# A Flamingo layer with an expert lookup: searches and decoding one stage ahead of the gather, and attention values as weights

## The reference, cut to what matters

```
x = x + tanh(g_xattn) * attention(layernorm(x), ctx, Wq, Wkv, Wout)      # causal softmax, 16 heads
x = x + tanh(g_ffn) * ffn(layernorm(x), ...)

h = silu(x W_up + b_up) W_down + b_down                                  # 256 -> 1024 -> 128
q = h W_q;  sim = q . keys                                               # 2 x 8 heads x 45 keys
scores, idx = top_k(sim, 8)
sc, pk = top_k(sx[:, None] + sy[None, :], 8)                             # best 8 of 64 sums per head
indices = (ix * 45 + iy)[pk]                                             # 64 experts per token
z = silu((h . down_embed[indices]) * softmax(sc))
out = sum over the 64 of z * up_embed[indices]
```

## Time and profile before

| | |
|---|---|
| median of three runs | 1368.43 us |
| the profiled execution | 1370.69 us |
| its span on the core | 1368.9 us |
| PE busy | 1238.8 us, 90% |
| DVE busy | 1020.6 us, 75% |
| ACT busy | 653.0 us, 48% |
| POOL busy | 289.0 us, 21% |
| mean granted clock of PE | 0.955 of 2.4 GHz |

### The profile page before, as it was taken

The page is one execution under the profiler, slowest core; times in us unless marked ns, Lnnn a source line. Parts: engine busy times, 40 slices in busy tenths (PEclk is TensorE's granted clock), DMA queues, the critical chain, the costliest instruction groups (busy, mean ns, idle before and its releaser), DMA issues.

```text
span 1368.9 us, 47081 instructions
## 1 busy us (share of the span) xinstructions
PE 1238.8 (90%) x18876; PEld 1101.5 (80%) x18876; DVE 1020.6 (75%) x4298; ACT 653.0 (48%) x1866; POOL 289.0 (21%) x151
## 2 busy tenths in 40 slices
PE   5778999999999999999999999999999999999755
PEld 3666888888888888888888888888888888888644
DVE  1437878886787878778878787787888778877873
ACT  3455544554554455555454554554545545554210
POOL 1220222220122222112222220222222112222220
PEclk9989999999999999999999999999999999999968
DMA  7005433565542455555443565544345565444455
GB/s 188 6 6 130 119 91 74 120 134 134 134 122 83 75 124 134 134 134 122 106 116 65 130 134 133 134 114 112 98 81 134 134 134 129 110 112 86 106 124 123
DMA packets 300319, 153.30 MB, mean 112 GB/s; under 512 B 278111, under 2 KB 291271, under 8 KB 291911
## 3 DMA queue, kind: packets, MB, share of 16 engines
q1 hardware_dynamic: 300103, 150.29, 47.6%
HBM read 78.44 MB, written 4.72 MB: 61 GB/s over the span
## 4 chain that ended last, share of the span: by engine, by line
DVE 40%; PE 25%; DMA 21%; issue 11%; SPq 2%; ACT 1%; DVEq 0%; POOL 0%; POOLq 0%
DMA hot_rT<-expert_rows 16%; DVE uc L610 7%; PE bank L960 6%; DVE topi L702 6%; PE bank L841 4%; DMA expert_rows<-r_h 4%; DVE picked L589 3%; DVE besti L691 3%; DVE smax L617 3%; PE bank L854 2%; DVE best L682 2%; PE bank L910 2%; PE bank L864 2%; PE bank L891 2%; DVE eq L740 2%
## 5 line engine op out<-in xcount | busy, mean ns | idle before, releaser
L362 POOL TENSOR_TENSOR zl<-z 128x2048 f32<-128x2048 f32 x32 | 115.3, 3602 | 916.0 <-DVE uc L610 916.0
L1004 PE MATMUL bank<-ue,coef 128*128 128x256 f32 x1024 | 226.5, 379 | 1.4 <-ACT coef L418 1.4
L841 PEld LDWEIGHTS bank<-z,hot_rT 128*128 128x128 bf16 x2048 | 156.8, 96 | 72.1 <-DVE picked L589 26.9
L1004 PEld LDWEIGHTS bank<-ue,coef 128*128 128x128 f32 x1024 | 192.1, 190 | 26.4 <-ACT coef L418 1.6
L841 PE MATMUL bank<-z,hot_rT 128*128 128x32 bf16 x2048 | 167.4, 178 | 45.9 <-DVE picked L589 27.3
L602 DVE TENSOR_SCALAR hot_rT<-hot_rT,p_iota 128x4096 bf16<-128x4096 bf16 x64 | 82.3, 1286 | 161.2 <-DMA hot_rT<-expert_rows 161.2
L854 PE MATMUL bank<-uc,hot_r 128*128 128x32 bf16 x6144 | 164.5, 177 | 24.1 <-DVE uc L610 16.4
L854 PEld LDWEIGHTS bank<-uc,hot_r 128*128 128x128 bf16 x6144 | 161.5, 96 | 29.9 <-issue 29.3
L841 PE MATMUL bank<-zll,hot_rT 128*128 128x32 bf16 x2048 | 166.1, 177 | 3.4 <-issue 3.4
L841 PE MATMUL bank<-zl,hot_rT 128*128 128x32 bf16 x2048 | 166.1, 177 | 2.7 <-issue 2.7
L841 PEld LDWEIGHTS bank<-zl,hot_rT 128*128 128x128 bf16 x2048 | 157.7, 97 | 3.5 <-issue 3.5
(11 more groups left out here) (140 smaller groups left out, 2161.4 us busy)
## 6 DMA issues: line engine op xcount, KB each, us to landing
hot_rT<-expert_rows SPq DMA_DIRECT2D x64, 1024.0 KB, 6.2
xt<-in_x SPq DMA_DIRECT2D x32, 128.0 KB, 7.1
out<-x1k SPq DMA_DIRECT2D x32, 128.0 KB, 7.2
ue<-in_L_ffn_up_embed SPq DMA_DIRECT2D x1, 2048.0 KB, 16.3
ct<-in_ctx SPq DMA_DIRECT2D x32, 32.0 KB, 6.7
z<-in_L_ffn_W_up SPq DMA_DIRECT2D x1, 1024.0 KB, 8.8
expert_rows<-r_h SPq DMA_DIRECT2D x64, 8.0 KB, 1.8
hot_r<-hot_rT SPq DMA_TRANSPOSE x64, 8.2
```

Of the source, the lines that this page charges most:

```text
L362: nc.gpsimd.tensor_tensor(zl[:, side, :, :], z[:, side, :, :], top_half(z[:, side, :, :]), ALU.subtract).then_inc(S["zl_ok"], 1)
L841: last = mm(bG[k % 2][:, 32 * (q - 16 * k):32 * (q - 16 * k) + 32], hot_rT[:, q, :], part.rearrange("r (h q) c -> r h q c", h=2)[:, :, q, ...
L1004: last = mm(bG0[:, 0:DM], coef[:, c, :, :].rearrange("r h q -> r (h q)"), ue[:, c, :], start=(c == 0), stop=(c == C - 1))
```

## The change

It has three parts.

1. Stages. `topi`, `sums`, `best` and `besti` belong to the tile in `Fw`, at the end of its turn. The decoding belongs to stage `B`, now at the head of the turn. SP issues the spread of the row numbers and both DMA transposes in that same turn, and DVE's `hot_T` stands late in it. The gather of the next turn finds them there. `top_rep` and the exponential `ex` move on ACT to the head of the turn. POOL's split of `z` is done in `Fw`'s turn, after `sums_ok`, `xn2_ok` and `xn_ok`. The transposes of `sm_in` stand before the matmuls of L989 and write to the free half of bank `bT`.
2. Attention. The values (`v_diag`, now without its column of ones) are the weights, 32 columns of them, and `PT` moves: 16 matmuls of 64 columns, four after each other into four strips of 32 partitions of the bank (L956). Eight matmuls with `ones_diag` as weights give the sums of the probabilities, spread over the partitions (L960). The result is already transposed, so L990 and its copy on ACT go; DVE takes the reciprocal of 256 numbers in each partition (L694) in place of 16, and multiplies into `oT`.
3. Waits. `settled`, a semaphore nobody waits for, is no longer counted up behind some waits, and tile numbers are constants.

```diff
@@ SP
-                if Ct:
-                    Ct.free_apart("w_pe3")
-                    for part in range(2):
-                        qs = slice(part * Q // 2, (part + 1) * Q // 2)
-                        Ct.wait_apart(f"hotrT{part}")
-                        sp.dma_start_transpose(hot_r[:, qs, :], hot_rT[:, qs, :].rearrange("r q s -> r (q s)")).then_inc(S[f"hotr_in{part}"], 16)
...
+                    B.free("w_pe3")
+                    for part in range(2):
+                        qs = slice(part * Q // 2, (part + 1) * Q // 2)
+                        B.wait(f"hotrT{part}")
+                        sp.dma_start_transpose(hot_r[:, qs, :], hot_rT[:, qs, :].rearrange("r q s -> r (q s)")).then_inc(S[f"hotr_in{part}"], 16)
@@ POOL
-                    B.wait("z_sb3")
-                    B.free2("g_pe3")
-                    if Ct:
-                        Ct.wait("uc2")
...
+                    Fw.wait("z_sb3")
+                    Fw.free2("g_pe3")
+                    Fw.wait("sums_ok")
+                    if A:
+                        A.wait("xn2_ok")
+                    if L:
+                        L.wait("xn_ok")
@@ DVE
-                    hot_T(0)
...
-                    hot_T(1)
...
-                    nc.vector.reciprocal(rsum[:, :, :, :], av[:, :, :, HD:HD + 1]).then_inc(S["rs_ok"], 1)
+                    nc.vector.reciprocal(rsum[:, :, :], bD[:, 256:512].rearrange("d (a q) -> d a q", a=2)).then_inc(S["rs_ok"], 1)
...
+                    nc.vector.tensor_tensor(oT[:, :, :], bD[:, 0:256].rearrange("d (a q) -> d a q", a=2), rsum[:, :, :], ALU.mult).then_inc(S["o_ok"], 1)
...
+                if B:
+                    hot_T(0)
+                    hot_T(1)
@@ PE
-                    for s in range(2):
-                        for hp in range(8):
-                            last = mm(bD[64 * s:64 * s + 64, 34 * hp:34 * hp + 34], PT[:, hp, 64 * s:64 * s + 64],
-                                      v_diag[:, s, hp, :, :].rearrange("p o d -> p (o d)"), start=True, stop=True)
+                    for a in range(2):
+                        for s in range(2):
+                            for j in range(4):
+                                mm(bD[32 * j:32 * j + 32, 128 * a + 64 * s:128 * a + 64 * s + 64],
+                                   v_diag[:, s, 4 * a + j, :, :].rearrange("p o d -> p (o d)"), PT[:, 4 * a + j, 64 * s:64 * s + 64], start=True, stop=True)
+                    for a in range(2):
+                        for j in range(4):
+                            last = mm(bD[32 * j:32 * j + 32, 256 + 128 * a:384 + 128 * a], ones_diag[:, :, :].rearrange("p o d -> p (o d)"),
+                                      PT[:, 4 * a + j, :], start=True, stop=True)
```

More of the change, by code:

```diff
@@ L484, in turn @@
                     up_tanh(0)
+                if B:
+                    B.wait("dif_ok")
+                    B.free("p_ok")
+                    nc.scalar.activation(ex[:, :, :], dif[:, :, :], ACT.Exp).then_inc(S["ex_ok"], 1)
                 if A:
@@ L537, in turn @@
                 if B:
-                    B.wait("top_i")
-                    B.free("pick_ok")
-                    copy(top_rep[:, :, :, :], topi[:, :, :].rearrange("p l a -> p a l").unsqueeze(3).to_broadcast([128, K8, 2 * RH, K8]), "rep_ok")
-                    B.wait("dif_ok")
-                    B.free("p_ok")
-                    nc.scalar.activation(ex[:, :, :], dif[:, :, :], ACT.Exp).then_inc(S["ex_ok"], 1)
+                    B.wait("sm_pe")
+                    B.free2("hotc")
+                    for half in range(2):
+                        rows, cols = slice(half * 64, half * 64 + 64), slice(half * Q, half * Q + Q)
+                        src = bT[rows, 256:512].rearrange("p (n t) -> p n t", n=2)
+                        nc.scalar.activation(c_sm[rows, side, :, :], src[:, 0, cols].unsqueeze(2).to_broadcast([64, Q, 2]), ACT.Copy)
+                        last = nc.scalar.activation(p_sm[rows, side, :], src[:, 1, cols], ACT.Copy)
+                    last.then_inc(S["sm_ok"], 1)
                 if A:
@@ L986, in turn @@
                     scatter(2)
-                if A:
-                    A.wait("o_ok")
-                    for k in range(2):
-                        last = nc.tensor.transpose(bT[:, 128 * k:128 * k + 128], xn[:, 128 * k:128 * k + 128], ident[:, :])
-                    last.then_inc(S["oT_pe"], 1)
                 if Ct:
@@ L1000, in turn @@
                     dense(3)
+                if B:
+                    B.wait("rdup_ok")
+                    B.wait("p_ok")
+                    for n in range(2):
+                        last = nc.tensor.transpose(bT[:, 256 + 128 * n:384 + 128 * n], sm_in[:, n, :, :].rearrange("p a s -> p (a s)"), ident[:, :])
+                    last.then_inc(S["sm_pe"], 1)
                 if Ct:
@@ L1011, in turn @@
                     last.then_inc(S["x2T_pe"], 1)
-                if B:
-                    B.wait("rdup_ok")
-                    B.wait("p_ok")
-                    if Ct:
-                        Ct.wait("w_sb3")
-                    for n in range(2):
-                        last = nc.tensor.transpose(bG1[:, 128 * n:128 * n + 128], sm_in[:, n, :, :].rearrange("p a s -> p (a s)"), ident[:, :])
-                    last.then_inc(S["sm_pe"], 1)
             groups = list(weight_groups())
```

284 lines of the change are left out of this document (130 added, 154 removed), and 1 row of the table S.

## The result

The changed kernel takes 1285.49 us (median of 4 runs, 1282.74 to 1286.89), the kernel before 1368.76 us (1367.81 to 1371.82). The ratio is 0.9386, with a 95% interval of 0.9364 to 0.9407. The prediction said 1288, with 1262 to 1340 as its range. The profiled execution has a span of 1285.1 us.

A forecast was written before the change was run, and what follows sets the result against it. PE nearly fills each turn, with gather waits and clock falls behind them. Turn: 38.86 - 1.4 - 0.3 - 0.22 - 0.37 + 0.22 = 36.8, taken as 36.9; 160 + 1033 + 92 + 3 = 1288 us, range 1262 to 1340.

The forecast's parts named there:

- No wait for the spread: Before and inside the gather: row numbers arrive a stage earlier, so PE's waits of 0.43 and 1.0 go; gain 1.4 us.
- Attention values: Values and sums on PE: 1.77 us becomes 1.4 with overlapping strips, gain 0.37 a turn; bounds 1.3 and 3.5.
- Rival A: Attention values: the column strips don't overlap and cost 3.5 us, not 1.4; +67, 1355 us; chance 0.11.
- The scatter's wait: PE's wait before the scatter: DVE's uc starts earlier because sums no longer stands ahead of it; gain 0.3 us.
- L990 goes: Attention output: two transposes and their copy are dropped; gain 0.22 us a turn.
- sm_in: Its transposes leave the last hop and stand before the long matmuls with PE time of their own; cost 0.22 us.
- The reciprocal: DVE behind uc: 256 numbers take 1.95 us, 1.7 more than before; bounds 0.41 and 3.6.
- DVE busy 33.0: DVE's busy time in a full turn rises from 31.3 to 33.0 us of 36.7; DVE doesn't bind, but closely.
- POOL's splits needed at 6 us of the next turn: POOL's splits before the gather: they end 2 us into the next turn, with cover of 3 to 4 us.
- Rival D: No gain: another 2.5 us wait takes the place, such as POOL's split at twice its time; 1368 us; chance 0.03.
- rival B: PE's clock behind the gather still falls in 16 of 28 turns at 2.3 us each; +37, 1325 us; chance 0.12.
- Rival C: The output's DMA, behind the transposes, lands late and holds ACT's x1k; 1316 to 1411 us; chance 0.05.

The follow-up runs named there:

- e_stage: Changed kernel with its attention part undone (values moving, sums by a 17th column, output transposes, reciprocal of 16 numbers): 1295.29 us, ratio 0.9483.
- e_strip: Changed kernel with all attention products of one column strip before the next strip's, in place of the four strips in turn: 1291.98 us, ratio 0.9456.
- e_hold: Changed kernel with an extra, unread reciprocal of 256 numbers per partition on DVE ahead of the second picked product: 1354.39 us, ratio 0.9906.
- e_zl: Changed kernel with POOL's first subtraction zl moved a turn later, behind the last uc product: 1289.23 us, ratio 0.9418.
- e_pe: Changed kernel with the transposes of xn1 and ctx in another bank and the last embedding group ahead of the scatter: 1306.69 us, ratio 0.9566.
- e_fill: Changed kernel with three small DVE operations (sum and reciprocal of exponentials, cast into sm_in) moved into DVE's wait for tanh: 1282.27 us, ratio 0.9382.
- e_zlpe: Changed kernel with POOL's zl a turn later, xn1 and ctx transposed into another bank, and the last embedding group ahead of the scatter: 1263.39 us, ratio 0.9226.

## Why the prediction was right, and where it was not

The time came out 2.5 us below the forecast, and the mechanism was as forecast: the gather's waits went, and the falls of the clock with them. That the number is so close is partly luck. The values gained 0.38 us a turn more than their term, the gather 0.18 and L990's term 0.17; the scatter's wait came out 0.58 worse. The start was 3 us longer and the full turns together 5 us shorter than forecast. By PE's starts in the two turns laid out (38.83 and 36.59 from one L919 or L898 to the next) the steps are:

- *No wait for the spread* (1.4 forecast): up to the gather -0.50, inside it -1.08. Right in place, and 0.2 more. e_stage shows it without the attention part: 0.9483.
- *Attention values* (0.37 forecast): -0.75. Right in direction, mis-sized: I put the 64-column records at 27 ns, because the smallest matmuls took 26. Thirty-two of them went by in 0.47 us, 15 ns each. Rival A is out: taken in turn, the strips overlap. So is the bound of 3.5, even with one strip's work in a row (e_strip).
- *The scatter's wait* (-0.3 forecast): wrong. The stretch from L870 to L833 grew by 0.28. The faster values brought PE there 0.75 us sooner, DVE not: the gain of one term is the wait of the next. e_strip shows it from the other side.
- *L990 goes* (-0.22): from -0.39, with small waits in the scatter. *sm_in* (+0.22): 0.22.
- *The reciprocal* (1.95 us): 1.757, a slope of (1757 - 258)/240 = 6.2 ns a number. So "the trace agrees" was too kind to the other estimate of 2.1 us, which needs 8.3 ns. "DVE doesn't bind, but closely" held: 0.2 us of slack in e_hold, where I had counted on 2. The wait for POOL took most of the rest; without it DVE stands waiting for PE for 1.52 us (e_zl).
- *DVE busy 33.0*: 34.7. The term that was missing is the 1.5 us in which DVE's first operation with two SBUF operands waits for POOL's zll. I had looked only at whether POOL is in time. It cost nothing by itself (e_zl), but it had used up the cover I gave to the decoding ("1 us"): the first pick starts at 611.05, right where part 0 of the gather ends.
- *POOL's splits needed at 6 us of the next turn*: wrong by a turn. They end at 605.99, 2.1 us into the tile's turn in stage `B`, and its gather starts 5.8 us into the turn after that: some 40 us of cover, not 4. e_zl runs the two splits 26 and 33 us later, and PE doesn't wait for POOL. Rival D never was near.
- *The clock*: 1.00 in 28 of 28 turns, so rival B is out. The falls themselves are real: e_hold and e_pe bring them back with 1.4 and 1.0 us of waiting in the gather, at 1.4 and 1.2 us a fall.
- *Rival C*: the output lands in 2.1 us, not 3. ACT's wait fell from 25.7 to 2.9 us.
- *Start 160, last turns 92*: 163.2 and 91.2.

What I would not have got from my sum is how little the parts add. The attention part was priced at -0.59 a turn plus a reciprocal off the path. That has the right sign behind the staging (-0.34, a little over half), and the wrong one without it.

What bounds the turn now is a ring of two engines: PE from the scatter to the gather's first picks, DVE from there to uc, and beside it DVE's string from x1 through the decoding to the picks. e_fill, e_zl and e_pe each shortened one piece and gained nothing. e_zlpe shortened two and gained 22 us, as forecast from the ring before it ran.

## What to carry to other kernels

When two engines hand work to each other in a ring, an edit's own saving is not its price: time it with the edit that frees the other engine, and look at where the idle time goes. Here a wait of 1.0 us in the gather took the clock down in half of the turns, and the two gaps of 0.4 to 0.6 us that it replaced did not. Before moving work between DVE and POOL, list which of DVE's operations beside it read two tiles of SBUF. A transfer that nobody waits for can still be dear, if it fills the DMA engines over a long stretch: 3 MB a turn cost 118 us here.

## What the hardware showed that I had not expected

- The smallest DVE operation pays the whole wait for POOL: dif with 64 numbers took 1.82 us for 0.22, hot_c with 1024 took 2.28 for 0.69, and the cost moved from one to the other with their order.
- POOL waits as well: its `rstdb` on one number took 2.35 us for 0.55. It starts at 595.50 beside DVE's two `hot_rT` comparisons (595.34 to 597.81) and ends at 597.85.
- Float32 products on a strip of 32 columns: 15 ns a record of 64 columns and 34 ns a record of 128 when four strips take turns (0.47 us for 32, 0.55 for 16); together 1.02 us, and 1.76 with one strip's work in a row.
- PE stops of 3.1 to 4.7 us without a semaphore, when 5 MB of broadcasts and copies stand in the queue of one turn.
